# A macaron transformer block on one core: the expert routing computed in two parts, with weight sets behind the gather index

## The chip, the cores and the metric

The kernel runs on one core of one Trainium2 chip. The core has five engines that run beside each other, each through its own instructions in order: TensorE (PE; its weight loads are shown as PEld), VectorE (DVE), ScalarE (ACT), GpSimd (POOL) and SyncE (SP, which here issues transfers only). They meet through semaphores: an instruction increments one when it is done, and another engine waits for a value. The metric is the device time of one execution in microseconds, as a median of runs.

## What is computed

Input is x, 4 sequences of 512 tokens with 128 features, so 2048 tokens in 16 tiles of 128. Six stages follow, each on a layer-normed copy of x:

```python
x = x + 0.5 * ffn(layernorm(x))        # ternary weights, hidden size 512
x = x + attn0(layernorm(x))            # 16 heads of 64, causal, gated
x = x + 0.5 * ffn(layernorm(x))        # the same weights: "the last feed-forward"
x = x + 0.5 * moe(layernorm(x))        # the experts, first time
x = x + attn1(layernorm(x))
x = x + 0.5 * moe(layernorm(x))        # the experts, second time

def moe(X):                            # D = 128, 8 experts, hidden H = 512, top 2
    logits = X @ Wg + bg
    topv, topi = top_k(logits, 2)
    w = softmax(topv)                  # one weight for each of the two experts
    out = X
    for e in range(8):
        for s in range(2):
            xs = X * w[s]
            y = (silu(xs @ W1[e]) * (xs @ W3[e])) @ W2[e]
            out = out + where(topi[s] == e, y, 0)
    return out
```

## The kernel before

x stays in SBUF, tokens on the partitions. Matrix products are made in pairs of 16-bit halves: a number is split in a high and a low f16 part, and three products (high x high, high x low, low x high) are summed in PSUM; ScalarE writes the high parts and VectorE the low ones. PSUM has 8 banks, `ps[:, bank, :]`, of 512 f32 columns.

**Stages and their order.** Each engine has one program, written out by hand, and the order of its calls is the order of its work; no scheduler moves anything. The attention loops over 32 items (4 sequences of 8 head pairs) in 36 turns, as a pipeline of five steps: in turn t the item t is projected, t-1 has its row maxima, t-2 its scores, t-3 its outputs, t-4 its output projection. So turns 32 to 35 have less and less to do. A table `FILL` puts other work in the turns: the feed-forward of sequences 0 to 2 (`up`, `down`) and the router logits (`route(0, 0)`, `route(0, 1)`), and in the second attention `route(1, 0)` to `route(1, 2)`. What concerns the last sequence comes after the attention: `route(0, 2)`, the last feed-forward's `up(1, 3, k)` with VectorE's `hidden_low(1, 3, k)`, `down(1, 3)`, `x_ffn(1, 3)` (adds it to x), `stats(3, 3)`, `normed(3, 3)`, `turned_x(3, 3)` and `route(0, 3)`. After the second attention it is `stats(5, 3)` in turn 35, `normed(5, 3)`, `turned_x(5, 3)` and `route(1, 3)`. In an attention turn VectorE's `turned_low` (L1132) writes the low part of the turned outputs, which PE's `project_out` needs, and `add_out` (L1172) adds its result to x.

**The routing**, `moe(n, m)` on VectorE and `moe(m)` on PE, m = 0 and 1, begins when the logits and top two of all 16 tiles are there. All (token, expert) pairs, 4096, are sorted by expert, each expert's rows padded to whole tiles of 128; this gives up to 39 tiles of rows. The steps on VectorE are `hot` (one-hot of each choice, L1219) and `hoth` (sum of both, L1222); PE multiplies `hoth` by a triangular matrix and by ones and gives each pair's rank in its expert (bank 3) and each expert's count (bank 4). From the counts come the tiles of each expert (L1232 to L1240), from these and the ranks each pair's place (L1242 to L1250): a tile number and a row number in it. `in_row` (L1265) is the one-hot of the row number, `in_tile` the one-hot of the tile number in four versions: itself (L1253), times the token number (L1258), and times the high and low part of the weight (L1261). PE multiplies them (L1653) and gets in bank 5, for each row of each tile, the token, both weight parts and the choice. VectorE turns them into integer rows (`row_i[:, 0]`, the rows to gather, and `row_i[:, 1]`, the rows to scatter) and `wup`, the weights. `tile_ei` holds each tile's expert.

**The tiles.** GpSimd gathers 128 token rows per tile from HBM by an indirect transfer (L702), four ahead, and later scatters the result (L708), 8 tiles behind. PE loads the experts' offsets from `tile_ei` for eight tiles at once (L1663), transposes the gathered rows (L1674), multiplies by both expert matrices (L1366 to L1368), transposes the product (L1696) and multiplies by the third (L1708 to L1710). ScalarE copies the transposed rows (L926) and applies Silu (L932), after it has waited for `wup`.

Two helpers recur. `step(ins)` lets VectorE wait for the instruction just issued, as the next one reads its result:

```python
def step(ins):
    n[0] += 1
    ins.then_inc(chain, 1)
    eng.wait_ge(chain, n[0])
```

## Time and profile before

| | us |
|---|---|
| median of 3 runs | 1029.34 |
| lowest, highest | 1029.19, 1030.26 |
| the profiled execution | 1028.21 |
| its span, first to last instruction | 1026.4 |
| busy in the span: PE, DVE, POOL, ACT | 877.7, 791.5, 699.8, 615.5 |
| first routing, L1214 to L1285 on DVE | 399.05 to 419.08 |
| second routing, L1214 to L1285 on DVE | 882.49 to 902.44 |

The profile is of one execution. A row of the timeline has the start in us from the start of the span, the busy time, the engine, the line in the program, the operation, what it writes and reads, shapes, and how many like it follow each other (x2); in brackets how long the engine was idle before and who released it. The duration of a row with x2 is the busy time of both together.

### The profile page before, as it was taken

Reading aid. Unit: us, or ns where it says so; the run is one execution under the profiler, and the core shown is the slowest. Engines: PE = TensorE matmul, PEld = TensorE weight load, DVE = VectorE, ACT = ScalarE, POOL = GpSimd, SP = SyncE. Lnnn points to the kernel's source line nnn. Section 1 sums busy time; section 2 is a strip of 40 time slices with the busy share of each in tenths; the row PEclk is TensorE's granted clock in tenths of the full one; section 3 lists DMA queues with packets and bytes.
Section 4 is the critical chain, followed back from the end, with each engine's and each line's share of the span. In section 5 each row is a group of like instructions: output and inputs, shape, how many; then the busy total and the mean of one; then the engine's idle time right before and its main releaser. Section 6 shows DMA issues by size and latency. Waiting matters only on the chain.

```text
span 1026.4 us, 30792 instructions
## 1 busy us (share of the span) xinstructions
PE 877.7 (86%) x11902; PEld 615.0 (60%) x11902; DVE 791.5 (77%) x2348; ACT 615.5 (60%) x1024; POOL 699.8 (68%) x638
## 2 busy tenths in 40 slices
PE   5779999999999962699975899999999996189993
PEld 3447667767666641477752567667677665157772
DVE  6778988888889656577776988898888883757774
ACT  6578778778767620266643766666766663046661
POOL 5568899889887740377732887768877876057771
PEclk9899999999999976699996999999999998589997
DMA  4100011010030000111230000000000000011124
GB/s 149 52 34 29 17 44 43 3 43 3 2 103 4 3 11 11 23 53 53 52 103 5 2 2 3 2 12 2 13 3 2 12 3 1 11 36 52 53 50 139
DMA packets 29424, 31.75 MB, mean 31 GB/s; under 512 B 4130, under 2 KB 22306, under 8 KB 29284
## 3 DMA queue, kind: packets, MB, share of 16 engines
q1 hardware_dynamic: 23760, 19.29, 6.3%
q0 software_dynamic: 4992, 10.23, 3.8%
q8 instruction: 99, 1.62, 0.7%
q14 instruction: 41, 0.34, 0.1%
q10 hardware_dynamic: 532, 0.27, 0.1%
HBM read 21.52 MB, written 8.26 MB: 29 GB/s over the span
## 4 chain that ended last, share of the span: by engine, by line
PE 71%; DVE 15%; POOL 5%; ACT 4%; issue 3%; DMA 2%; SPq 0%; POOLq 0%; DVEq 0%; ACTq 0%
PE ps L1548 13%; PE ps L1366 8%; PE ps L1367 8%; PE ps L1368 8%; PE ps L1554 4%; PE ps L1696 3%; PE ps L1571 3%; PE ps L1572 3%; PE ps L1573 3%; PE ps L1516 3%; POOL arena L676 3%; DVE arena L1114 2%; PE ps L1581 2%; PE ps L1708 2%; PE ps L1709 2%
## 5 line engine op out<-in xcount | busy, mean ns | idle before, releaser
L676 POOL TENSOR_TENSOR arena<-arena 128x1024 f16<-128x1024 f32 (+1 forms) x192 | 347.6, 1811 | 106.0 <-ACT arena L843 95.6
L835 ACT ACTIVATE arena<-ps 128x1024 f32<-128x1024 f32 (+1 forms) x192 | 169.2, 881 | 137.3 <-PE ps L1554 136.9
L1114 DVE CUSTOM_DVE_ANT_0 arena<-ps,mask_qk 128x512 bf16<-128x512 f32 (+3 forms) x512 | 224.7, 486 | 23.2 <-PE ps L1516 18.2
L1548 PE MATMUL ps<-arena 64*128 64x512 f16 (+3 forms) x1536 | 149.7, 301 | 11.7 <-ACT arena L835 8.0
L1571 PE MATMUL ps<-arena 128*128 128x65 f16 x1280 | 130.4, 195 | 5.5 <-POOL arena L676 5.5
L702 POOL DMA_INDIRECT arena<-x_rows,arena x78 | 76.5, 980 | 82.3 <-DVE arena L1285 52.6
L1572 PE MATMUL ps<-arena 128*128 128x64 f16 x1280 | 130.5, 194 | 0.0
L1573 PE MATMUL ps<-arena 128*128 128x65 f16 x1280 | 130.2, 194 | 0.0
L1571 PEld LDWEIGHTS ps<-arena 128*128 128x128 f16 x1280 | 118.5, 98 | 5.9 <-POOL arena L676 5.9
L1573 PEld LDWEIGHTS ps<-arena 128*128 128x128 f16 x1280 | 118.0, 98 | 0.0
L1572 PEld LDWEIGHTS ps<-arena 128*128 128x128 f16 x1280 | 117.8, 99 | 0.0
L674 POOL CAST arena<-arena 128x1024 f16<-128x1024 f32 (+1 forms) x128 | 107.2, 838 | 0.0
L708 POOL DMA_INDIRECT y_rows<-arena x78 | 76.8, 985 | 34.9 <-issue 20.1
L1548 PEld LDWEIGHTS ps<-arena 64*128 64x128 f16 x1536 | 57.0, 94 | 65.6 <-ACT arena L835 26.5
L1301 DVE SCALAR_TENSOR_TENSOR arena<-ps,arena 128x512 f32<-128x512 f32 x78 | 58.5, 750 | 36.7 <-ACT arena L932 29.5
L1548 PE MATMUL ps<-arena,sel 64*128 64x512 f16 (+3 forms) x512 | 77.5, 299 | 0.0
L1516 PE MATMUL ps<-arena 64*128 64x512 f16 (+3 forms) x512 | 67.5, 301 | 11.2 <-DVE arena L1114 10.7
L932 ACT ACTIVATE arena<-ps,arena 128x512 f32<-128x512 f32 x78 | 53.7, 689 | 29.8 <-PE ps L1368 29.8
L1307 DVE TENSOR_TENSOR arena<-ps,arena 128x512 f16<-128x512 f32 x78 | 54.0, 692 | 18.6 <-ACT arena L938 18.6
L843 ACT ACTIVATE arena<-arena 128x1024 f16<-128x1024 f32 x64 | 67.4, 1052 | 0.0
L938 ACT ACTIVATE arena<-ps 128x512 f16<-128x512 f32 x78 | 46.6, 597 | 32.2 <-PE ps L1696 32.2
L1554 PE MATMUL ps<-mask_kq,identb 128*128 128x128 bf16 x512 | 62.4, 225 | 0.0
(254 smaller groups left out, 2580.4 us busy)
## 6 DMA issues: line engine op xcount, KB each, us to landing
stage<-in_L_ffn_W SPq DMA_DIRECT2D x4, 1024.0 KB, 5.5
arena<-y_rows SPq DMA_DIRECT2D x16, 256.0 KB, 4.8
x_rows<-XN SPq DMA_DIRECT2D x8, 256.0 KB, 2.3
arena<-x_rows,arena POOLq DMA_INDIRECT x78, 2.5
y_rows<-arena POOLq DMA_INDIRECT x78, 2.3
stage<-in_L_attn_Wkv SPq DMA_DIRECT2D x2, 512.0 KB, 7.9
out_x<-X SPq DMA_DIRECT2D x4, 256.0 KB, 2.9
X<-in_L_attn_tokens SPq DMA_DIRECT2D x3, 256.0 KB, 5.2
```

The source lines that it names most:

```text
L674: g.tensor_copy(PH[:, b, :, cols], P32[:, :, cols]).then_inc(s_ph_pool, 1)
L676: g.tensor_tensor(PL[:, b, :, cols], P32[:, :, cols], PH[:, b, :, cols], ALU.subtract).then_inc(s_pl, 1)
L835: a_.activation(P32[:, :, UNIT_AT[u]:UNIT_AT[u] + UNIT_W[u]], ps[:, 4:6, 0:UNIT_W[u]], ACT.Exp).then_inc(s_ex_p, 1)
L1114: v_.tensor_tensor_reduce(masked[:, x, 0:w], ps[:, 2 + x, at:at + w], mask_qk[:, CH - w:CH], 1.0, NEG, ALU.add, ALU.max, accum_out=MX[:, i ...
L1366: mm(dst, sh, mh, start=True, stop=False)
L1367: mm(dst, sh, ml, start=False, stop=False)
L1516: ins_ = mm(ps[:, 2 + x, at:at + (i + 1) * P], QKh[rows, r, 0, i * P:(i + 1) * P], QKh[rows, r, 1, 0:(i + 1) * P], start=(n_ == 0), stop=( ...
L1548: mm(ps[:, 4 + x, at:at + w], keys, queries, start=(n_ == 0 and part == 0), stop=False)
L1554: ins_ = mm(ps[:, 4 + x, at:at + P], identb[:], mask_kq[:], start=False, stop=(n_ == len(EXP_UNITS[u]) - 1))
L1571: mm(ps[:, 6 + x, c:c + DH + 1], ph_, VH[:, r, k, x, 0:DH + 1], start=(k == 0), stop=False)
L1572: mm(ps[:, 6 + x, c:c + DH], ph_, VL[:, r, k, x, :], start=False, stop=False)
L1573: ins_ = mm(ps[:, 6 + x, c:c + DH + 1], pl_, VH[:, r, k, x, 0:DH + 1], start=False, stop=(k == i))
```

## The change

The 16 tiles are split in EARLY = 12 (three sequences) and TPC = 4 (the last sequence). One-hots, ranks within the expert and the row matrices of the first 12 are computed before the last sequence is routed. To make that possible the row number is taken from the rank alone (rank and 127), and the expert's first tile is added to the tile number afterwards (`first`, `tile_h`). The early part of the first routing lies around the last feed-forward, that of the second in turns 32 to 34 of the second attention. Behind the last sequence's route come its own one-hots, ranks and rows and the two remaining versions of `in_tile`, then the index to gather. The weight versions of `in_tile`, their product (32 matmuls of its own, bank 6) and the rows to scatter now stand behind that index; GpSimd waits for the scatter rows (`s_r_home`) before its first scatter. `in_row` and the small tiles of the early part move to a place in the arena that the attention does not use.

The diff, cut to its core (the functions are also printed above as they were):

```diff
 # GpSimd, scatter(t)
+                    if t == 0:
+                        pool.wait_ge(s_r_home, m + 1)
 # VectorE, attention, end of a turn
+                    if a == 1 and t == ITEMS:
+                        experts_of(0, EARLY)
+                    if a == 1 and t == ITEMS + 2:
+                        early_ranks(1)
+                        rows_of(1, 0, EARLY)
+                        rows_of(0, 0, EARLY)
 # VectorE, new functions
+            def experts_of(lo, hi):
+                for j in range(TOPK):
+                    ins_ = v_.tensor_copy(idxf[:, j, lo:hi], idx8[:, lo:hi, j])
+                step(ins_)
+                for j in range(TOPK):
+                    ins_ = v_.tensor_tensor(hot[:, j, lo:hi], iota_e[:, lo:hi],
+                                            idxf[:, j, lo:hi].unsqueeze(2).broadcast_to([P, hi - lo, EXPERTS]),
+                                            ALU.is_equal)
+                step(ins_)
+                v_.tensor_tensor(hoth[:, lo:hi], hot[:, 0, lo:hi], hot[:, 1, lo:hi], ALU.add).then_inc(s_r_hot, 1)
+            def ranks_of(lo, hi, rank):
+                step(v_.tensor_tensor(prod[:, :, lo:hi].rearrange("p j t e -> p j (t e)"),
+                                      rank.unsqueeze(1).broadcast_to([P, TOPK, (hi - lo) * EXPERTS]),
+                                      hot[:, :, lo:hi].rearrange("p j t e -> p j (t e)"), ALU.mult))
+                step(v_.tensor_reduce(posf[:, :, lo:hi], prod[:, :, lo:hi], AX.X, ALU.add))
+                step(v_.tensor_copy(posi[:, :, lo:hi], posf[:, :, lo:hi]))
+                v_.tensor_scalar(at_i[:, 0, :, lo:hi], posi[:, :, lo:hi], int(math.log2(P)), None, ALU.logical_shift_right)
+                step(v_.tensor_scalar(at_i[:, 1, :, lo:hi], posi[:, :, lo:hi], P - 1, None, ALU.bitwise_and))
+                for k in range(2):
+                    ins_ = v_.tensor_copy(at_h[:, k, :, lo:hi], at_i[:, k, :, lo:hi])
+                step(ins_)
+            def rows_of(j, lo, hi):
+                return v_.tensor_tensor(in_row[:, j * NT + lo:j * NT + hi, :],
+                                        row_no[:].unsqueeze(1).broadcast_to([P, hi - lo, P]),
+                                        at_h[:, 1, j, lo:hi].unsqueeze(2).broadcast_to([P, hi - lo, P]), ALU.is_equal)
+            def early_ranks(m):
+                dve.wait_ge(s_r_rank, 2 * m + 1)
+                ranks_of(0, EARLY, ps[:, 3, 0:EARLY * EXPERTS])
 # VectorE, moe: after the tile totals (in place of L1240 to L1265)
+                ranks_of(EARLY, NT, ps[:, 4, 0:TPC * EXPERTS])
+                for j in (1, 0):
+                    rows_of(j, EARLY, NT)
+                flat = [P, TOPK * NT, EXPERTS]
+                step(v_.tensor_tensor(prod.rearrange("p j t e -> p (j t) e"), hot.rearrange("p j t e -> p (j t) e"),
+                                      cnt[:, 3, :].unsqueeze(1).broadcast_to(flat), ALU.mult))
+                step(v_.tensor_reduce(first, prod, AX.X, ALU.add))
+                step(v_.tensor_tensor(tile_h, at_h[:, 0], first, ALU.add))
+                half = [P, NT, ETILES]
                 for j in (1, 0):
                     blk = slice(j * NT, (j + 1) * NT)
+                    step(v_.tensor_tensor(in_tile[:, blk, 1, :], tile_no[:].unsqueeze(1).broadcast_to(half),
+                                          tile_h[:, j].unsqueeze(2).broadcast_to(half), ALU.is_equal))
+                    v_.tensor_tensor(in_tile[:, blk, 0, :], in_tile[:, blk, 1, :],
+                                     token_1[:].unsqueeze(2).broadcast_to(half), ALU.mult).then_inc(s_r_row, 1)
...
                 dve.wait_ge(s_r_sum, m + 1)
+                step(v_.tensor_scalar(row_f[:, 0, :], ps[:, 5, 0:ETILES], -1.0, 0.0, ALU.add, ALU.max))
+                v_.tensor_copy(row_i[:, 0, :], row_f[:, 0, :]).then_inc(s_r_index, 1)
+                step(v_.tensor_tensor(wts[:, 3, :], wts[:, 1, :], wts[:, 2, :], ALU.mult))
+                step(v_.tensor_copy(wh_r[:, 0], wts[:, 2:4, :]))
+                step(v_.tensor_tensor(wh_r[:, 1], wts[:, 2:4, :], wh_r[:, 0], ALU.subtract))
+                for k in range(2):
+                    v_.tensor_tensor(in_tile[:, :, 2 + k, :], in_tile[:, :, 1, :], w_r[:, k].unsqueeze(2).broadcast_to(every),
+                                     ALU.mult).then_inc(s_r_wset, 1)
...
+                v_.tensor_copy(row_i[:, 1, :], row_f[:, 3, :]).then_inc(s_r_home, 1)
+                dve.wait_ge(s_r_wsum, m + 1)
 # VectorE, between the first attention and moe(3, 0)
             route(0, 2)
+            experts_of(0, EARLY)
             for k in range(FB):
                 hidden_low(1, 3, k)
+            early_ranks(0)
+            rows_of(1, 0, EARLY)
             x_ffn(1, 3)
             stats(3, 3)
             normed(3, 3)
+            rows_of(0, 0, EARLY)
             turned_x(3, 3)
 # PE: early_ranks(1) at the end of turn 33, early_ranks(0) before down(1, 3), early_counts(m) before turned_x
+            def early_ranks(m):
+                pe.wait_ge(s_r_hot, 2 * m + 1)
...
+            def early_counts(m):
...
 # PE, moe
+                pe.wait_ge(s_r_wset, TOPK * (m + 1))
+                for b in range(TOPK * NT):
+                    ins_ = mm(ps[:, 6, 0:2 * ETILES], in_row[:, b, :], in_tile[:, b, 2:4, :].rearrange("p a b -> p (a b)"),
+                              start=(b == 0), stop=(b == TOPK * NT - 1))
+                ins_.then_inc(s_r_wsum, 1)
                 pe.wait_ge(s_r_tile, m + 1)
```

Three places show how the instructions stand. VectorE, from the last `hidden_low` (a low half of the hidden layer, 128x512 x4) to the transposed norm's low part `XTl`, before:

```order
L998 SCALAR_TENSOR_TENSOR arena<-ps,arena 128x512 x4
L1013 SCALAR_TENSOR_TENSOR X<-ps,X 128x512
L975 BN_STATS bst<-X 128x6 x4
L978 BN_AGGR mv<-bst 128x2 x4
L1005 TENSOR_SCALAR XN<-X,mv,rstd 128x128 x4
L992 TENSOR_TENSOR XTl<-ps,XTh 128x512
```

and with the change:

```order
L1007 SCALAR_TENSOR_TENSOR arena<-ps,arena 128x512 x4
L1241 TENSOR_TENSOR arena<-ps,arena 128x2x96
L1244 TENSOR_REDUCE arena<-arena 128x2x12
L1245 CAST arena<-arena 128x2x12
L1246 TENSOR_SCALAR arena<-arena 128x2x12
L1247 TENSOR_SCALAR arena<-arena 128x2x12
L1249 CAST arena<-arena 128x2x12 x2
L1253 TENSOR_TENSOR arena<-row_no,arena 128x1536
L1022 SCALAR_TENSOR_TENSOR X<-ps,X 128x512
```

Seven instructions of ranks and one row matrix now stand ahead of `x_ffn(1, 3)` (X<-ps,X).

VectorE, turns 34 and 35 of the second attention: reciprocal and scaled outputs of the last item, `add_out`, `turned_low`, `add_out`; before:

```order
L1156 RECIPROCAL arena<-ps 128x8
L1160 TENSOR_TENSOR arena<-ps,arena 128x2x4x64
L1172 SCALAR_TENSOR_TENSOR X<-ps,X 128x512
L1132 TENSOR_TENSOR arena<-ps,arena 128x512
L1172 SCALAR_TENSOR_TENSOR X<-ps,X 128x512
L975 BN_STATS bst<-X 128x6 x4
```

and with the change:

```order
L1181 SCALAR_TENSOR_TENSOR X<-ps,X 128x512
L1241 TENSOR_TENSOR arena<-ps,arena 128x2x96
L1244 TENSOR_REDUCE arena<-arena 128x2x12
L1245 CAST arena<-arena 128x2x12
L1246 TENSOR_SCALAR arena<-arena 128x2x12
L1247 TENSOR_SCALAR arena<-arena 128x2x12
L1249 CAST arena<-arena 128x2x12 x2
L1253 TENSOR_TENSOR arena<-row_no,arena 128x1536 x2
L1141 TENSOR_TENSOR arena<-ps,arena 128x512
L1181 SCALAR_TENSOR_TENSOR X<-ps,X 128x512
```

The ranks and both early row matrices stand between the two `add_out`, ahead of the last `turned_low`.

PE, the end of the routing up to the first transposed token tiles, before:

```order
L1647 MATMUL ps<-arena,onesh 128x8 x16
L1653 MATMUL ps<-arena 128x156 x16
L1653 MATMUL ps<-arena 128x117 x16
L1663 TENSOR_LOAD arena
L1674 MATMUL ps<-ident,arena 128x128 x2
```

and with the change:

```order
L1718 MATMUL ps<-arena 128x78 x16
L1718 MATMUL ps<-arena 128x39 x16
L1724 MATMUL ps<-arena 128x78 x32
L1733 TENSOR_LOAD arena
L1744 MATMUL ps<-ident,arena 128x128 x2
```

The 32 weight matmuls are new, and stand ahead of the load of the expert offsets and of the first transpose.

## Rows read from the trace of the kernel before

**Rows 1.** The page: granted clock in 40 slices of the span, tenths of full.

```profile
PEclk9899999999999976699996999999999998589997
```

**Rows 2.** Waits from 395 to 425: who waited for whom, us in total, times, longest.

```profile
POOL arena L702 <- DVE arena L1285: 26.4, 1, 26.4
```

**Rows 3.** Timeline of DVE, the second routing (start, busy time, engine, line, operation).

```profile
882.49 0.19 DVE L1214 TENSOR_TENSOR arena<-top 128x16 f32<-128x16 f32 x1
...
883.41 0.29 DVE L1222 TENSOR_TENSOR arena<-arena 128x128 f16<-128x128 f32 x1
...
885.40 0.17 DVE L1232 TENSOR_SCALAR arena<-ps 128x8 f32<-128x8 f32 x1 [0.68 <-PE ps L1647]
...
886.93 0.17 DVE L1240 TENSOR_SCALAR arena<-arena 128x8 f32<-128x8 f32 x1
...
890.80 1.53 DVE L1258 TENSOR_TENSOR arena<-arena,token 128x624 f16<-128x624 f16 x2
892.25 2.82 DVE L1261 TENSOR_TENSOR arena<-arena 128x1248 f16<-128x1248 f16 x2
894.98 4.49 DVE L1265 TENSOR_TENSOR arena<-row_no,arena 128x2048 f16<-128x2048 f16 x2
899.39 0.48 DVE L1269 TENSOR_TENSOR arena<-tile_no,arena 128x312 f32<-128x312 f16 x1
...
901.32 0.32 DVE L1278 COPY arena<-ps 128x156 f32<-128x156 f32 x1 [0.51 <-PE ps L1653]
...
902.44 0.18 DVE L1285 CAST arena<-arena 128x39 int32<-128x39 f32 x1
```

**Rows 4.** Timeline of PE, the second routing.

```profile
883.75 0.29 PE L1641 MATMUL ps<-arena,before 128*128 128x128 f16 x1 [2.84 <-DVE arena L1222]
...
897.33 3.96 PE L1653 MATMUL ps<-arena 128*128 128x156 f16 x32 [12.04 <-DVE arena L1265]
```

**Rows 5.** Timeline of all engines, from the second routing's first gather.

```profile
902.90 1.11 POOL L702 DMA_INDIRECT arena<-x_rows,arena  x1 [26.28 <-DVE arena L1285]
...
905.67 0.48 PE L1674 MATMUL ps<-ident,arena 128*128 128x128 f32 x1 [4.39 <-DMA arena<-x_rows,arena]
906.25 0.28 ACT L926 ACTIVATE arena<-ps 128x128 f16<-128x128 f32 x1 [23.32 <-PE ps L1674]
...
907.15 0.64 PE L1366 MATMUL ps<-E1h,arena 128*128 x1
```

**Rows 6.** The load of the expert offsets: min/median/max ns, first and last start.

```profile
L1663 PEldq TENSOR_LOAD <-arena x10: 589/594/1071, 417.5 to 980.9; - x10
```

**Rows 7.** Timeline of DVE, from the last hidden_low to the first routing.

```profile
386.93 0.69 DVE L998 SCALAR_TENSOR_TENSOR arena<-ps,arena 128x512 f16<-128x512 f32 x1 [0.30 <-ACT arena L761]
389.75 0.69 DVE L1013 SCALAR_TENSOR_TENSOR X<-ps,X 128x512 f32<-128x512 f32 x1 [2.13 <-PE ps L1391]
...
393.23 1.12 DVE L1005 TENSOR_SCALAR XN<-X,mv,rstd 128x128 f32<-128x128 f32 x4 [1.47 <-POOL rstd L590]
396.25 0.69 DVE L992 TENSOR_TENSOR XTl<-ps,XTh 128x512 f16<-128x512 f32 x1 [1.90 <-ACT XTh L751]
...
399.05 0.19 DVE L1214 TENSOR_TENSOR arena<-top 128x16 f32<-128x16 f32 x1
```

**Rows 8.** Timeline of PE, first expert matmul of the first routing.

```profile
424.45 0.64 PE L1366 MATMUL ps<-E1h,arena 128*128 x1
```

**Rows 9.** Timeline of DVE, turns 34 and 35 of the second attention.

```profile
870.27 0.69 DVE L1172 SCALAR_TENSOR_TENSOR X<-ps,X 128x512 f32<-128x512 f32 x1 [0.35 <-PE ps L1368]
871.55 0.69 DVE L1132 TENSOR_TENSOR arena<-ps,arena 128x512 f16<-128x512 f32 x1 [0.59 <-ACT arena L862]
```

**Rows 10.** Busy time by stretch: length, PE, PEld, DVE, ACT, POOL, granted clock, DMA share, GB/s.

```profile
874.00:880.00 6.00, 1.12 (x4) 0.72 (x4) 2.65 (x13) 0.60 (x1) 1.27 (x2) 0.50 0.15 44
430.00:432.00 2.00, 2.00 (x13) 1.32 (x13) 1.49 (x3) 1.36 (x3) 0.95 (x1) 0.95 0.00 0
910.00:912.00 2.00, 2.00 (x8) 0.75 (x8) 0.95 (x2) 0.83 (x2) 1.20 (x2) 0.63 0.14 35
```

117 lines of the change are left out of this document (54 added, 63 removed).

## The prediction

> **What bounds the kernel now.** I read the times first: 1029.34 us is the median, the profiled execution took 1028.21 us with a span of 1026.4, so differences of the trace are taken off the median unscaled. Next the row of the granted clock over 40 slices: it dips at slices 17 to 19 and 35 to 37, the two places where the experts are routed, once after each attention [rows 1]. The waits around the first one then name who is late: POOL stands 26.4 us before its first gather and is released by DVE's index cast [rows 2]. The timeline of DVE at the second routing shows why. From the first instruction of the routing (L1214, 882.49) to the index cast (L1285, 902.44) DVE hardly pauses: 19.95 us of one chain, in which the two row matrices take 4.4 us and the 32x39 weight sets 2.7 [rows 3]. PE has two bursts in it and otherwise waits for DVE [rows 4]. Then come gather, transpose, ScalarE's copy, and the first expert matmul (L1366) at 907.15, 24.66 after the start [rows 5]. In the first routing the same span is 399.05 to 424.45, or 25.40 [rows 7, 8]. From the first expert matmul on PE has work without end; so what counts in each routing is when that matmul starts, against what is added ahead of L1214.
>
> **The new chain on DVE, T = 0 at L1214.** Durations fit 0.16 us plus one element per 0.96 GHz cycle, in f16 and f32 alike: 8 elements 0.17, two of 624 elements 1.53 together, two of 2048 elements 4.49 [rows 3]. An instruction that waits for the one before adds 0.03; one that doesn't starts some 0.1 before the last one's end.
> - One-hots of one sequence instead of four: the sum matrix is issued at 0.70 (before 0.92) and ends at 0.89. PE starts 0.15 later and has 8 small matmuls in place of 32. From PE's start to DVE's reading 32 matmuls took 1.65 [rows 3, 4]; 8 take a quarter and a little for the fixed part, 0.5: DVE reads the counts at 1.5, before at 2.91. Adding one and the reciprocal end at 1.3 and hide.
> - Tile totals: L1232 to L1240 took 1.53 [rows 3]; the scaling by 128 is gone: 3.04.
> - Ranks of the last sequence: product and sum over 64 elements, 0.26 each, cast 0.21, shift and mask 0.30, two casts 0.30: 1.33, to 4.4.
> - Two row matrices of 512 elements, 0.69 long, 0.62 apart: 1.24, to 5.6. The other 1536 elements of each are elsewhere (below).
> - First tile of each expert: two operations on 256 elements at 0.46 and an add of 0.20: 6.7.
> - Membership: per half 624 elements, 0.84 with its wait, and the token product 0.73 (two of 624 took 1.53 [rows 3]): 3.14, to 9.9. PE multiplies the second half, 16 matmuls of 39 columns, in under 1 us beside what comes next, so DVE's 0.5 wait for the sum goes.
> - Tile experts: from L1269 to the wait before L1278 it was 1.42 [rows 3], the last of which overlaps: to 11.2. Then one operation straight from PSUM and the cast: the index is cast at 11.4 against 19.95, and POOL starts its gather at 11.9 against 20.4 [rows 5]. That is 8.5 us earlier.
>
> **What is queued behind the index.** The first expert matmul does not get these 8.5 us, because the weight sets now stand between. On DVE: three small steps (0.63) from 11.5, two products of 1248 elements (2.83 together, [rows 3]): 15.0. On PE 32 matmuls of 78 columns stand ahead of everything of the tiles. At 1.2 GHz, where 16 of 156 and 16 of 117 columns took 3.96 [rows 4], they need 32 x 0.065 = 2.1: last start 17.1. Behind them in PE's queue is the load of the expert offsets, which took 0.59 to 1.07 [rows 6] and was hidden behind the gather; now it is bare. I take 0.7: transpose of token tile 0 at 17.8. The gather, 2.8 from issue to transpose [rows 5], arrives at 14.7 and is hidden; the second, issued some 1.4 behind it, also. DVE meanwhile makes the scatter rows (0.9), reads the weight sum at 17.4 and is ready at 18.1, when ScalarE may start; the transpose releases it at 17.8 + 0.58 = 18.4. From ScalarE's copy to the first expert matmul 0.90 [rows 5]: 19.3. The gains are 25.40 - 19.3 = 6.1 and 24.66 - 19.3 = 5.4, in all **11.5**. The scatter's new wait on POOL is met: its rows are ready at 16, and the first scatter comes eight gathers later.
>
> **What the moved part costs, first routing.** The early one-hots (0.9) lie between route(0, 2) and the first hidden_low, where DVE waits for ScalarE. PE's 12 early rank matmuls (some 0.5) fit in where it waits for the last hidden_low, and the 24 early count matmuls fall where PE waits for the norm. But DVE's early ranks (product and reduction over 192 elements 0.40 each, the rest 0.82: 1.62) and the first row matrix of 1536 elements (1.67 to the next start) stand between the last hidden_low and x_ffn(1, 3). DVE is free at 387.55 and x_ffn started at 389.75 [rows 7]; now at 387.55 + 3.3 = 390.85. **Cost 1.1**, on the path (x_ffn, statistics, norm, transpose, route). The second matrix of 1.76 falls between the norm's end, 394.3, and turned_x at 396.25 [rows 7]: it just fits. If that cover were gone it would cost up to 1.7 more.
>
> **Second routing.** The early one-hots fit after turn 32. But the rest is issued after add_out of turn 34, and in-order DVE then has 1.62 + 2 x 1.67 = 5.0 ahead of turned_low(31), the last output tile of the last head pair. add_out started at 870.27 and the next can start at 870.9; turned_low started at 871.55 [rows 9]. New: 875.9. **Cost 4.3**, all on the path, since PE's last projection, add_out, statistics and norm follow one from the other. And PE stands idle for those 4.3; its projection moves from before 874 to about 876.6, and from 874 on the clock was at its lower level [rows 10]. Its 12 matmuls of 128 columns then run at 1.2 GHz and not at 2.4: 12 x 0.053 = **0.6** more, 0 if the clock holds or was low already.
>
> **The clock at the first tiles.** In 430 to 432 the granted clock is 0.95 and in 910 to 912 it is 0.63 [rows 10], so it rose to 2.4 GHz at 430.2 and 911.5: 5.75 and 4.35 us after the first expert matmul. All of it ran at half speed. Now the weight matmuls and two transposes run up to 1 us before that matmul. Bounds: nothing counts and both ramps last 5.75, a loss of 0.7; or the clock is up when the tiles begin, a gain of (5.75 + 4.35)/2 = 5.0. I take the mean ramp begun 1 us earlier, half a microsecond in each routing: **1.0**.
> The Trainium skill (TensorE: Matmul & The Clock Gate, What's actually happening) says that the gate follows how busy the array has lately been. By that rule alone the weight matmuls should warm the array and the 5.0 be nearer. The trace is divided: a burst of the same kind, 3.96 us long, was followed by pure waiting for the gather and the tiles began at half speed both times.
>
> **Sum.** 11.5 - 1.1 - 4.3 - 0.6 + 1.0 = 6.5 us: 1029.34 - 6.5 = **1022.8 us**.
>
> **Rivals.**
> - Warm start: the clock is high within half a microsecond of the first tiles. For it, PE now works from 15.0 on with gaps below 1 us; against it, the spread of the two ramps seen. 1029.34 - 5.5 - 5.0 = 1018.8.
> - The tail block is hidden: if something else holds turned_low(31), or the block slides into DVE's earlier waits of turns 33 and 34, the 4.9 goes: 1018. Against it, the queue is in order and the block stands behind add_out.
> - The early part is real but small: the first tile is still held by something that did not move, as the serial weight path being 2.5 us longer in each routing (offset load at its longest 1.07, a second wait on the sum, products slower while PE reads the same tiles). Then about half of the 11.5 stays, against 6.0 of cost: 1028.5.
> - Slower: the 32 weight matmuls stand in PE's queue ahead of every tile. In the rows a matmul lasts 0.31 but the next one starts after 0.13 at 156 columns, which is why I price them at 0.065. If 64 of them went one after the other at 0.31, that is 15.7 more: 1038.5. It decides from 0.065 + 6.5/64 = 0.17 a matmul on. Only the rows of the longer matmuls speak against it.
>
> **How the numbers follow.** Forecast 0.78 (1020.5 to 1026), warm start 0.12, hidden tail 0.03, small gain 0.04, slower 0.03. Each DVE chain may be off by 0.7, 1.4 in all; with the clock at its worst (1.7 below my value) the end above is 1026, and the warm start sets the end below, 1019. By 0.2%, 2.06 us, about what a measurement of this kernel can tell from no change: faster 0.93, within 0.04, slower 0.03.
>
> **What would show it.** The index cast 11.4 after the routing's first DVE instruction instead of 19.95; the first expert matmul 19.3 after it in both routings; a bare offset load of 0.6 to 1.1 behind the weight matmuls; x_ffn(1, 3) later by 1.1; a block of 5.0 on DVE between the last two outputs of the second attention, with PE idle beside it; the clock's rise under 5 us after the first expert matmul. It is wrong if the block is not on the path, if the weight matmuls are more than 0.1 apart, or if the tiles begin at 2.4 GHz.

## Result and profile after

The changed kernel takes 1022.81 us (median of 4 runs, 1020.87 to 1023.76) where the kernel before takes 1029.26 (4 runs, 1028.93 to 1030.26) on the same chip: a ratio of 0.9933, 95% interval 0.9916 to 0.9951. The forecast was 1022.8. Its profiled execution has a span of 1022.0 us, before 1026.4. The kernel was run again later, as f0: 1021.48 against 1029.14, ratio 0.9932 (0.9916 to 0.9947), span 1019.5.

Cut at the same events in each trace, the span divides as follows (T is the first DVE instruction of a routing, L1214 before and L1263 after; all in us, one execution each):

| stretch | before | after | f0 |
|---|---|---|---|
| start to the last hidden_low of the last feed-forward | 386.93 | 387.88 | 386.45 |
| to T of the first routing | 12.12 | 13.15 | 13.15 |
| to the first expert matmul | 25.40 | 18.83 | 18.83 |
| expert tiles, to DVE's last result | 103.01 | 102.22 | 102.16 |
| to DVE's first L1114 (after: L1123) of the second attention | 25.91 | 26.01 | 25.93 |
| to its fourth last add_out | 299.41 | 300.83 | 300.84 |
| to its second last add_out | 17.49 | 16.99 | 16.96 |
| to T of the second routing | 12.22 | 17.07 | 17.07 |
| to the first expert matmul | 24.66 | 18.75 | 18.76 |
| expert tiles, to DVE's last result | 102.27 | 102.11 | 102.07 |
| to the end of the span | 16.96 | 18.17 | 17.28 |

The rows behind it follow. First the page's granted clock in 40 slices, after; it answers to [rows 1]. The dips of the two routings lie at slices 15 to 17 and 35 to 36, before at 15 to 17 and 34 to 36 (the prediction counted them two slices too late, at 17 to 19 and 35 to 37), and they are about as deep as they were. The dip at slices 21 and 22 is the start of the second attention.

```profile
PEclk9899999999999986699987999999999999579997
```

The timeline of DVE after, first routing (start, busy time, engine, line, operation, and in brackets what ended the idle time before it). It answers to [rows 3], which is the second routing; the two run alike within 0.1.

```profile
401.03 0.19 DVE L1263 TENSOR_TENSOR arena<-top 128x16 f32<-128x16 f32 x1
...
402.53 0.17 DVE L1271 TENSOR_SCALAR arena<-ps 128x8 f32<-128x8 f32 x1 [0.23 <-PE ps L1710]
...
412.38 0.18 DVE L1306 CAST arena<-arena 128x39 int32<-128x39 f32 x1
...
413.13 2.83 DVE L1314 TENSOR_TENSOR arena<-arena 128x1248 f16<-128x1248 f16 x2
...
418.31 0.20 DVE L1323 COPY arena<-ps 128x39 f32<-128x39 f32 x1 [1.41 <-PE ps L1724]
...
418.77 0.24 DVE L1325 TENSOR_SCALAR arena<-arena 128x39 f32<-128x39 f32 x1
```

The counts are read 1.50 after T, and the index is cast at 11.35 (11.28 in the second routing, where it was 19.95). The weight sets (L1314) stand behind the cast, and the weight is ready (L1325 ends) at 17.98.

The timeline of the other engines, from the first gather to the first expert matmul, first routing, after. It answers to [rows 4, 5, 8].

```profile
412.87 1.24 POOL L709 DMA_INDIRECT arena<-x_rows,arena  x1 [17.70 <-DVE arena L1306]
...
416.01 2.26 PE L1724 MATMUL ps<-arena 128*128 128x78 f16 x32 [4.34 <-DVE arena L1314]
...
418.07 0.67 PE L1744 MATMUL ps<-ident,arena 128*128 128x128 f32 x2
...
419.05 0.45 ACT L935 ACTIVATE arena<-ps 128x128 f16<-128x128 f32 x2 [17.59 <-DVE arena L1325]
...
419.86 0.60 PE L1408 MATMUL ps<-E1h,arena 128*128 x1 [1.12 <-DVE arena L1331]
```

The gather is issued 5.2 before the transpose (L1744) needs it and is hidden. What releases ScalarE is now DVE's weight, no longer the transpose as in [rows 5]. The load of the expert offsets, to be compared with [rows 6] (min/median/max ns, first and last start):

```profile
L1733 PEldq TENSOR_LOAD <-arena x10: 591/598/1073, 416.9 to 975.4; - x10
```

It starts at 416.9 and, even at its longest, is over by 418.0, while the weight matmuls still run to 418.27. The transposes start directly behind them.

DVE from the last hidden_low to the second row matrix, after, answers to [rows 7]:

```profile
387.88 0.69 DVE L1007 SCALAR_TENSOR_TENSOR arena<-ps,arena 128x512 f16<-128x512 f32 x1 [0.46 <-ACT arena L770]
...
390.06 1.76 DVE L1253 TENSOR_TENSOR arena<-row_no,arena 128x1536 f16<-128x1536 f16 x1
391.74 0.68 DVE L1022 SCALAR_TENSOR_TENSOR X<-ps,X 128x512 f32<-128x512 f32 x1
...
396.24 1.75 DVE L1253 TENSOR_TENSOR arena<-row_no,arena 128x1536 f16<-128x1536 f16 x1
398.23 0.69 DVE L1001 TENSOR_TENSOR XTl<-ps,XTh 128x512 f16<-128x512 f32 x1 [0.23 <-ACT XTh L760]
```

x_ffn (L1022) follows hidden_low by 3.86, before by 2.82. It no longer waits for PE. The second matrix fits with 0.24 to spare.

DVE at the end of the second attention, after, answers to [rows 9]; the last row is PE's, the first matmul of the last output projection.

```profile
865.91 0.68 DVE L1181 SCALAR_TENSOR_TENSOR X<-ps,X 128x512 f32<-128x512 f32 x1
...
868.08 3.43 DVE L1253 TENSOR_TENSOR arena<-row_no,arena 128x1536 f16<-128x1536 f16 x2
871.42 0.68 DVE L1141 TENSOR_TENSOR arena<-ps,arena 128x512 f16<-128x512 f32 x1
...
873.66 0.69 DVE L1181 SCALAR_TENSOR_TENSOR X<-ps,X 128x512 f32<-128x512 f32 x1 [1.56 <-PE ps L1410]
```

```profile
872.16 0.29 PE L1408 MATMUL ps<-WOh,arena 128*128 128x128 f16 x1 [5.46 <-DVE arena L1141]
```

Five microseconds without a pause, and turned_low (L1141) behind them with no wait of its own: this block of ranks and row matrices (the tail block below) is late, nothing else. PE stood idle for 5.46 before its projection.

Busy time by stretch (length, PE, PEld, DVE, ACT, POOL, granted clock, DMA share, GB/s), after; it answers to [rows 10]. The rows are the two ramps (a ramp is the time from the first expert matmul until the clock is at 2.4 GHz) and the projection's window.

```profile
424.00:426.00 2.00, 2.00 (x12) 1.08 (x11) 0.75 (x1) 1.21 (x3) 0.21 (x2) 0.88 0.11 33
904.00:906.00 2.00, 2.00 (x8) 0.75 (x7) 0.95 (x2) 0.30 (x2) 0.94 (x1) 0.56 0.01 2
870.00:874.00 4.00, 1.84 (x32) 1.84 (x33) 2.44 (x3) 0.00 (x0) 0.00 (x0) 0.50 0.01 4
```

The clock rises to 2.4 GHz at 424.5 and 905.8, that is 4.6 and 4.0 after the first expert matmul. In 870 to 874 it is 0.50 throughout; before it was 0.93 in the same window.

### The profile page after: what moved, and what is told of

Same layout as the page of the kernel before. It is cut to its first block, busy times and chain, and to the rows that moved or that the text cites. A ratio compares the mean times of both kernels' runs of the same rounds, so it can differ in the third digit from the quotient of the medians.

```text
span 1022.0 us, 31003 instructions
## 1 busy us (share of the span) xinstructions
PE 876.2 (86%) x11990; PEld 615.3 (60%) x11990; DVE 799.2 (78%) x2382; ACT 615.0 (60%) x1024; POOL 700.3 (69%) x638
## 3 DMA queue, kind: packets, MB, share of 16 engines
q8 instruction: 100, 1.64, 0.6%
## 4 chain that ended last, share of the span: by engine, by line
PE 70%; DVE 15%; POOL 5%; ACT 4%; issue 3%; DMA 2%; SPq 1%; POOLq 0%; DVEq 0%; ACTq 0%
PE ps L1590 12%; PE ps L1408 8%; PE ps L1409 8%; PE ps L1410 8%; PE ps L1596 4%; PE ps L1766 3%; PE ps L1613 3%; PE ps L1614 3%; PE ps L1615 3%; PE ps L1558 3%; POOL arena L683 3%; DVE arena L1123 2%; PE ps L1623 2%; PE ps L1779 2%; PE ps L1778 2%
## 5 line engine op out<-in xcount | busy, mean ns | idle before, releaser
L1123 DVE CUSTOM_DVE_ANT_0 arena<-ps,mask_qk 128x512 bf16<-128x512 f32 (+3 forms) x512 | 224.6, 486 | 24.1 <-PE ps L1558 19.3
L1339 DVE SCALAR_TENSOR_TENSOR arena<-ps,arena 128x512 f32<-128x512 f32 x78 | 58.5, 750 | 38.1 <-ACT arena L941 31.1
L1558 PE MATMUL ps<-arena 64*128 64x512 f16 (+3 forms) x512 | 67.3, 300 | 12.5 <-DVE arena L1123 12.0
```

What stands on the lines that cost most here:

```text
L1123: v_.tensor_tensor_reduce(masked[:, x, 0:w], ps[:, 2 + x, at:at + w], mask_qk[:, CH - w:CH], 1.0, NEG, ALU.add, ALU.max, accum_out=MX[:, i ...
L1558: ins_ = mm(ps[:, 2 + x, at:at + (i + 1) * P], QKh[rows, r, 0, i * P:(i + 1) * P], QKh[rows, r, 1, 0:(i + 1) * P], start=(n_ == 0), stop=( ...
```

## Experiments

All kernels are derived from the changed one. Two chips were used. The first four runs went to a chip on which the kernel before takes 1063.65 us (17 runs), the other six to one where it takes 1029.14 (11 runs; 1028.55 over 8 runs beside the last two). Times are compared by the ratio to the kernel before on the same chip. The changed kernel without an edit was not run on the first chip, so for e4, e5, e1 and e6 its ratio of 0.9933 is carried over from elsewhere, and the main readings rest on distances inside the traces. What the first chip does differently is told under the last heading.

**e4: the split kept, nothing early.** The early part is computed inside the routing, ahead of the last sequence's part, on DVE and on PE.

```diff
-                    if a == 1 and t == ITEMS + 2:
-                        early_ranks(1)
-                        rows_of(1, 0, EARLY)
-                        rows_of(0, 0, EARLY)
...
+                experts_of(0, EARLY)
+                early_ranks(m)
+                rows_of(1, 0, EARLY)
+                rows_of(0, 0, EARLY)
                 experts_of(EARLY, NT)
```

> The same split and the same instructions, but the part of the first 12 tiles is computed at the start of the routing, after the last route, and not beside other work. Theory A, the gain is in hiding that part: one-hots 0.9, ranks 1.6, row matrices 3.4 and a round trip to TensorE of about 0.7 come back, so the first expert matmul is 25.3 us after the routing's first instruction against 18.8; 13 us more in two routings, less the 1.1 and 4.9 that the early part cost elsewhere: 1022.8 + 7 = 1029.8. Rival B, the gain came from putting the weight sets behind the gather index: at most 1025.

Measured: 1066.05 us (10 runs), ratio 1.0024 (1.0011 to 1.0036). The index is cast 18.10 and 18.03 after T, and the first expert matmul comes 25.81 and 25.63 after it. The two costs are gone: x_ffn again 2.82 behind hidden_low, and 12.42 from the second last add_out to T. Theory A put the first expert matmul at 25.3 and the time 7 us above the changed kernel; by the ratios it is 9.7. In the traces the two routings take 13.5 more (against e1) and x_ffn and the end of the attention give 5.7 back, which is 7.8; the other 2 us were not looked for. So the gain is the work moved out of the chain, less what it costs where it was put. Splitting and putting the weights behind the index, without moving anything out, bring nothing; they cost 0.24%.

**e5: the weight sets ahead of the gather index, as before.** The early part stays early.

```diff
+                step(v_.tensor_tensor(wts[:, 3, :], wts[:, 1, :], wts[:, 2, :], ALU.mult))
...
+                    v_.tensor_tensor(in_tile[:, :, 2 + k, :], in_tile[:, :, 1, :], w_r[:, k].unsqueeze(2).broadcast_to(every),
+                                     ALU.mult).then_inc(s_r_wset, 1)
+
                 step(v_.tensor_tensor(tile_e8, tile_no[:].unsqueeze(2).broadcast_to([P, ETILES, EXPERTS]),
```

> The changed kernel with the weight sets computed ahead of the tile experts and of the gather index on VectorE, as in the kernel before. Theory A, in the changed kernel the first tile is released by the weights and not by the gather: the index cast moves from 11.4 to 14.9 us after the routing's start, the gather starts at 15.3, its second transfer lands at 19.7 and the first expert matmul starts at about 19.9 instead of 18.8, so 1.1 us more in each routing: 1025. Rival B, the index was the gain: 3.5 us more in each: 1029.8.

Measured: 1058.39 us (4 runs), ratio 0.9959 (0.9943 to 0.9975). The index falls back by 3.4 (14.75 and 14.67 after T), the weight comes 1.8 earlier, and the first expert matmul is at 20.09 and 19.38 against 19.03 and 18.92 on the same chip with the changed order (e1): 1.1 and 0.5 later, where theory A had 1.1 twice. Timeline of e5, first routing:

```profile
415.86 1.24 POOL L709 DMA_INDIRECT arena<-x_rows,arena  x1 [21.10 <-DVE arena L1315]
...
416.91 0.18 DVE L1326 TENSOR_SCALAR arena<-arena 128x39 f32<-128x39 f32 x1
...
418.62 0.47 PE L1745 MATMUL ps<-ident,arena 128*128 128x128 f32 x1 [2.42 <-DMA arena<-x_rows,arena]
```

Here the weight is ready at 417.1 and PE waits 2.42 for the gathered rows. The two orders hold the first tile by different chains, and they differ by only 0.5 to 1.1, since the gather's 2.8 and the weight's path through PE are of like length. The changed order is the better one because its gather is fully hidden.

**e1: the tail block moved half a turn forward.** In turn 34 ranks and both row matrices go ahead of evacuate, behind the turned_low before.

```diff
+                    if a == 1 and t == ITEMS + 2:
+                        early_ranks(1)
+                        rows_of(1, 0, EARLY)
+                        rows_of(0, 0, EARLY)
                     if v is not None:
                         evacuate()
```

> The changed kernel with one block moved: in turn 34 of the second attention the early ranks and both early row matrices stand ahead of the evacuation of the last item's outputs, where VectorE waited 5.9 us, and no longer behind add_out. Theory A, the block of 4.9 us was on the path and its idle time also put the last projection on the low clock (0.6): from add_out(30) to the first instruction of the routing it takes 12.2 us as before the change, not 17.1, and the kernel takes 1022.8 - 4.9 = 1017.9. Rival B, something else held the last turned_low, so the block was free: 1022.8. Rival C, the block now runs beside GpSimd's subtraction of the exponentials and stretches it, as the 1.95 us cast in turn 32 shows the two engines disturbing each other: the last outputs come up to 2 us later, 1020.

Measured: 1052.69 us (5 runs), ratio 0.9909 (0.9894 to 0.9925) where the changed kernel has 0.9933 and 0.9932: about half of theory A's 4.9. From the fourth last add_out to T it is 30.53 instead of 34.06, so 3.5 come back; against the kernel before (29.71) 0.8 are missing. The timeline of DVE and one row of PE in e1:

```profile
879.06 3.43 DVE L1253 TENSOR_TENSOR arena<-row_no,arena 128x1536 f16<-128x1536 f16 x2
882.40 0.20 DVE L1165 RECIPROCAL arena<-ps 128x8 f32<-128x8 f32 x1
```

```profile
883.39 0.66 PE L1623 MATMUL ps<-ident,arena 128*128 128x128 f32 x4 [2.27 <-DVE arena L1169]
```

The block ends, evacuate (L1165) begins without a wait, and PE stands 2.27 for it (0.36 in the changed kernel). The granted clock belongs to this reading. In e1 it was 1.00 from 873.9 to 884.1, and PE had the last item's outputs ready 14.7 after the fourth last add_out, while the block ended at 16.6: 2.0 late. Before the change most of that turn ran at 0.50 and the outputs were ready at 16.2; there the same block would be 0.4 late (an estimate from these two). Behind it the clock of e1 was 0.50, and the last add_out came 2.25 after turned_low (before 1.62). That 0.63, and 0.18 of a longer wait for ScalarE ahead of turned_low, are the missing 0.8; the second last add_out lies 17.49 behind the fourth last in both. Rival C is not what is seen: GpSimd's tensor instruction at the start of the block takes 1.15 with and without it beside.

**f1: the block spread, and the first routing's row matrix moved.** One row matrix of the second routing goes behind the norm; in the first routing one goes behind the statistics instead of ahead of x_ffn.

```diff
+                        early_ranks(1)
+                        rows_of(1, 0, EARLY)
                     if v is not None:
                         evacuate()
...
-            rows_of(1, 0, EARLY)
             x_ffn(1, 3)
             stats(3, 3)
+            rows_of(1, 0, EARLY)
...
             normed(5, 3)
+            rows_of(0, 0, EARLY)
             turned_x(5, 3)
```

> The changed kernel with its early part spread over VectorE's waits: in the second attention the early ranks and one row matrix stand ahead of the last evacuation (turn 34) and the other behind normed(5, 3); around the last feed-forward the first row matrix stands behind stats(3, 3) and no longer ahead of x_ffn(1, 3). Theory A: from add_out(30) to the routing it takes 12.2 to 12.5 us as before the change (17.1 changed), from the last hidden_low to the routing 12.3 (13.1 changed, 12.1 before); 5.5 us less than the changed kernel of this call. Rival B, POOL's work is stretched by VectorE's beside it: half of that, 2 to 3.

Measured: 1018.70 us (5 runs), ratio 0.9901 (0.9885 to 0.9916), span 1015.0 against 1019.5 of f0. Theory A's 5.5 was missed: by the medians it is 2.8, as in rival B (the profiled execution of f1 was the lowest of its five). At the tail 5.46 come back (28.57 from the fourth last add_out to T, f0 34.03, before 29.71), which is more than the block cost. The same edit in f3 and g1 gives 29.78 and 29.87, so 4.2 are the block's, and T is as far from that add_out as before the change. The other 1.2 of f1 are the clock's: where its dip falls in the last turns is not the same. In f3 DVE waits 1.44 for PE behind the smaller block; in f1, with turn 34 at full clock as in e1, it does not wait and is 0.3 late. Busy time by stretch in turn 34, of f1 and then of f3:

```profile
862.00:864.00 2.00, 1.66 (x45) 1.48 (x41) 1.97 (x3) 0.00 (x0) 0.00 (x0) 1.00 0.00 0
```

```profile
860.00:862.00 2.00, 2.00 (x39) 2.00 (x37) 0.61 (x1) 0.00 (x0) 0.00 (x0) 0.50 0.00 0
```

The first routing loses, though. x_ffn is early again (2.88), yet T comes 13.59 after hidden_low where f0 has 13.15. The timeline of f1 shows why:

```profile
391.38 1.73 DVE L1252 TENSOR_TENSOR arena<-row_no,arena 128x1536 f16<-128x1536 f16 x1
391.55 1.64 POOL L594 TENSOR_SCALAR pw<-mv 128x4 f32<-128x4 f32 x1 [11.79 <-DVE mv L987]
```

POOL's 4-element step ends 0.08 after the row matrix beside which it runs, and the norm waits for it.

**g1: f3 (below) with that one matrix put back ahead of x_ffn.** This tests that reading.

```diff
+            rows_of(1, 0, EARLY)
             x_ffn(1, 3)
             stats(3, 3)
-            rows_of(1, 0, EARLY)
```

> The kernel of f3 with one thing undone: in the first routing the 1536-element row matrix stands ahead of x_ffn(1, 3) again, as in the changed kernel (spread in turn 34 and filler matmuls stay). Theory A, that the row matrix beside POOL's computation of the norm is what cost f1 and f3 0.45 us there: POOL's L594 falls from 1.64 to 0.22, the first routing starts 13.15 after the last hidden_low instead of 13.60, and the time is 0.4 us under f3, 1012.6 where before is 1029.1 (ratio 0.9844), which is less than the intervals can part; the trace has to show it. Rival B, that POOL's 1.64 has another cause: it stays and the routing starts at 13.6 plus the 1.04 that the matrix costs ahead of x_ffn, 14.6, and the time is 1014.

Measured: 1013.12 us (4 runs), ratio 0.9851 (0.9833 to 0.9870), f3 0.9848. The times can't part the two, as expected; the trace does. T is 13.15 after hidden_low (f3 13.60), and the same POOL step in g1 takes:

```profile
393.59 0.22 POOL L594 TENSOR_SCALAR pw<-mv 128x4 f32<-128x4 f32 x1 [12.95 <-DVE mv L987]
```

So it is 1.64 with a row matrix beside it and 0.22 without, as theory A had it. The Trainium skill (SBUF — State Buffer, SBUF: two separate sides) says that VectorE and GpSimd share a pair of ports as an exclusive lock, which a VectorE instruction with two SBUF inputs holds to its end against a GpSimd instruction that reads SBUF. The row matrix has two such inputs, and the ends 0.08 apart agree with it.

**e6: PE kept busy ahead of the weight matmuls.** Nine matmuls of 512 columns whose result nobody reads (fillers below) stand between the token sums and PE's wait for the weight sets.

```diff
+                for _ in range(9):
+                    mm(ps[:, 2, :], XTh[:, 0:P], XTh[:, 0:CH], start=True, stop=True)
                 pe.wait_ge(s_r_wset, TOPK * (m + 1))
```

> The changed kernel with nine extra matmuls of 512 columns on TensorE, between the token sums and the weight matmuls, where it waited 4.3 us for the weight sets; their result is not used. Theory A, what the array did lately decides the clock: weight matmuls and tiles begin at 2.4 GHz, which gives back half of the 4.6 and 4.0 us that the tiles ran at 1.2 GHz and about 1 us at each set of weight matmuls: 1022.8 - 6.3 = 1016.5. Rival B, the clock rises only some 4 us after the tiles begin, whatever came before: 1022.8. In between, it rises within the tiles earlier than before: 1019 to 1021.

Measured: 1056.40 us (6 runs), ratio 0.9930 (0.9910 to 0.9949), as the changed kernel and as rival B had it, but not for its reason: the clock rose at 414.6 and was lost again. PE and DVE of e6, first routing, and busy time by stretch behind it:

```profile
416.37 1.30 PE L1726 MATMUL ps<-arena 128*128 128x78 f16 x32 [1.04 <-DVE arena L1314]
...
419.00 0.20 DVE L1323 COPY arena<-ps 128x39 f32<-128x39 f32 x1 [1.75 <-PE ps L1726]
...
420.50 0.39 PE L1408 MATMUL ps<-E1h,arena 128*128 x1 [2.00 <-DVE arena L1331]
```

```profile
420.00:422.00 2.00, 1.50 (x6) 0.81 (x7) 0.49 (x2) 1.97 (x3) 1.17 (x2) 0.86 0.24 31
422.00:424.00 2.00, 2.00 (x6) 0.60 (x5) 0.95 (x2) 0.54 (x3) 0.95 (x1) 0.50 0.10 35
```

The weight matmuls take 1.30 instead of 2.26, but DVE does not read their sum earlier: 1.3 after PE's modelled end. After 2.0 without work the expert matmuls begin at full speed (0.39), and the clock falls under them at about 421.4 and is 0.50 until after 424.

**f2: PE kept busy in all three of its waits.** Nine such matmuls (warm(n) issues n of them), and four more behind the weight matmuls and four ahead of the first expert matmul.

```diff
+                warm(9)
                 pe.wait_ge(s_r_wset, TOPK * (m + 1))
...
                 ins_.then_inc(s_r_wsum, 1)
+                warm(4)
...
                     k, e = t % 2, offsets[t]
+                    if t == 0:
+                        warm(4)
```

> The changed kernel with unused matmuls of 512 columns in all three of TensorE's waits behind the token sums: nine before the weight matmuls, four behind them, four behind the two token transposes ahead of the first expert matmul. With nine alone the clock did rise, at 414.6, but fell again at 421.4 behind 2.0 us of idling, so that 4 us of the tiles still ran at 1.2 GHz. Theory A, without that gap the clock stays at 2.4 GHz through the first tiles: (4.6 + 4.0)/2 = 4.3 us less than the changed kernel of this call, less 0.5 if the last four overlap the first tile. Rival B, the clock falls whatever fills the gap: no gain, up to 1 us lost.

Measured: 1017.68 us (5 runs), ratio 0.9898 (0.9883 to 0.9914). The first expert matmul comes 0.67 earlier in both routings (18.16, 18.09), and the tiles take 100.68 and 100.46 instead of 102.16 and 102.07 (f0). PE of f2, first routing:

```profile
414.10 1.29 PE L1728 MATMUL ps<-arena 128*128 128x78 f16 x32 [1.18 <-DVE arena L1314]
415.23 1.02 PE L1724 MATMUL ps<-XTh 128*128 128x512 f16 x4
...
416.31 1.03 PE L1724 MATMUL ps<-XTh 128*128 128x512 f16 x4
417.27 0.39 PE L1408 MATMUL ps<-E1h,arena 128*128 x1
```

The granted clock is 1.00 from 413 to 426 without a break. That is a gain of 4.4 in the two routings, where theory A had 4.3; the median shows 3.8.

**g2: the four and four alone, without the nine.**

```diff
-                warm(9)
                 pe.wait_ge(s_r_wset, TOPK * (m + 1))
```

> The changed kernel with 4 unused 512-column matmuls behind the weight matmuls and 4 ahead of the first expert matmul, and not the 9 ahead of the weight matmuls. PE then has work without a gap from the weight matmuls on (416.0 in the first routing), at half clock at first. Theory A, that the clock rises some 4 us after the start of unbroken work whatever it is (in f2 2.5 to 4 us behind the first filler, in the changed kernel 4.0 and 4.6 behind the first expert matmul): it rises at 419.5 to 420.5, at or just behind the first expert matmul, the loops take 101.0 to 101.4 instead of 102.1; the fillers at half clock (0.43 each) end at about 420.3 and so hold the first expert matmul 0.4 us back; whole gain over the changed kernel 0.8 to 1.8 us, about 1020 where before is 1029.1. Rival B, that the clock must be up before the gap to be held through it: it rises as in the changed kernel 4 us after the first expert matmul, and the time is 1022 to 1023, with the fillers' 0.4 lost twice.

Measured: 1022.58 us (5 runs), ratio 0.9944 (0.9930 to 0.9959): nothing gained, and neither theory is right as a whole: the time is rival B's, the clock is theory A's. PE of g2, first routing:

```profile
415.35 2.26 PE L1727 MATMUL ps<-arena 128*128 128x78 f16 x32 [4.34 <-DVE arena L1314]
417.41 1.91 PE L1724 MATMUL ps<-XTh 128*128 128x512 f16 x4
419.11 0.63 PE L1748 MATMUL ps<-ident,arena 128*128 128x128 f32 x2
419.54 1.41 PE L1724 MATMUL ps<-XTh 128*128 128x512 f16 x4
420.79 0.38 PE L1408 MATMUL ps<-E1h,arena 128*128 x1
```

The clock did what theory A said: PE worked without a pause from 415.35, the clock was up at 420.3, ahead of the first expert matmul, and the tiles take 100.60 and 100.30. But the eight fillers make that matmul not 0.4 but 1.58 and 1.32 late: at half clock the first four hold the transposes until 419.1, and the next four wait behind those. Tiles gain 1.56 and 1.77, the start loses 2.90. In f2, behind the nine, the same four and four take 1.02 and 1.03, and the first expert matmul is not late at all.

**f3: f1 and f2 together.** The edits are those of both.

> Both of the two before together. The parts do not touch each other: by theory A of both 5.5 + 4 = 9.5 us less than the changed kernel of this call. If only the spread works, 5.5; if they disturb each other, less than the larger of the two.

Measured: 1013.02 us (5 runs), ratio 0.9848 (0.9831 to 0.9865), span 1011.3. That is 16.1 under the kernel before and 8.5 under the changed one on the same chip (f1 alone gives 2.8, f2 alone 3.8, by medians), where theory A had 9.5.

**f0: the changed kernel again**, without an edit, beside f1 to f3. Its numbers stand under the result.

> The changed kernel itself, beside the others of this call. On the chip of the first experiments the kernel before took 34 us more than on that of the first result, and from the first expert matmul to the last result each expert phase took 119 us in place of 102. Theory A, the gain does not depend on the chip, since neither DVE's chain nor the attention's end differ: 6.5 us less than the kernel before here too. Rival B, it shrinks or grows where the expert loop is slower: outside 5 to 8.

It is 7.7 us less than the kernel before, inside 5 to 8. But this chip runs the kernel before in the same time as the first result's (1029.14 and 1029.26), so rival B, which speaks of a chip with slower expert loops, was not tested.

## Why the prediction was right, and where it was right by luck

- **The chain to the index** held closely: counts at 1.50 (forecast 1.5), index cast at 11.35 (11.4). The work that e4 puts back into it costs 6.7 of the index and 6.8 and 6.7 of the first expert matmul (against e1, on the same chip).
- **Which chain holds the first tile** was right: the weights, not the index. e5 shows it from the other side.
- **First expert matmul:** forecast 19.3, measured 18.83 and 18.75, so the gains are 6.57 and 5.91, in all 12.5 and not 11.5. The mis-sized term is the offset load. The prediction laid it bare behind the weight matmuls at 0.7, so that the transpose would be at 17.8 and ScalarE would start at 18.4. It ran beside them: the transpose started at 17.04, and ScalarE at 18.02, right behind DVE's weight (17.98), forecast at 18.1. So what released ScalarE was the weight, and not the transpose as forecast. The 32 weight matmuls took 2.26 in all (forecast 2.1), so the rival that they stand 0.17 or more apart falls.
- **x_ffn:** forecast 1.1, measured 1.04, and T moved by 1.03. The second matrix fitted as forecast.
- **The tail block:** forecast 4.3 + 0.6. turned_low came 5.51 instead of 1.28 after add_out, which is 4.23, and the next add_out 2.24 instead of 1.62 after it, which is 0.62, with the projection's matmuls 0.10 apart at a granted clock of 0.50. In f3 T is 29.78 behind the fourth last add_out, before 29.71: without the block nothing of it is left.
- **The ramps:** forecast 1.0; the clock rises 4.6 and 4.0 (f0: 4.4 and 4.0) after the first expert matmul where it took 5.75 and 4.35, and the tiles take 0.95 (f0: 1.05) less. The price of a microsecond at half clock, 0.5 in the prediction, was too high: the 4.4 and 4.0 of f0 cost 1.5 and 1.6 of tile time against f2. The prediction's other bound, a warm start, did not come by itself. The weight matmuls did not warm the tiles. The rule that the prediction took from the Trainium skill (TensorE: Matmul & The Clock Gate, What's actually happening), that the gate follows how busy the array has lately been, is borne out by f2, though: with PE at work through the waits the two loops take 4.1 less than before the change, and the first expert matmuls come 1.3 earlier than in the changed kernel, against the 5.0 of that bound.
- **A miss without consequence:** the early one-hots after turn 32 took 3.8 and not 0.9. Timeline of DVE and of POOL, after:

```profile
849.51 1.95 DVE L1230 CAST arena<-idx 128x12 f32<-128x12 uint32 x2
851.49 0.72 DVE L1233 TENSOR_TENSOR arena<-iota_e,arena 128x96 f32<-128x96 f32 x2
852.25 1.09 DVE L1237 TENSOR_TENSOR arena<-arena 128x96 f16<-128x96 f32 x1
```

```profile
849.22 2.13 POOL L683 TENSOR_TENSOR arena<-arena 128x1024 f16<-128x1024 f32 x1
...
852.01 1.21 POOL L683 TENSOR_TENSOR arena<-arena 128x512 f16<-128x512 f32 x1
```

In the first routing, with POOL idle, the same three took 0.25, 0.43 and 0.26. Here the casts end 0.11 after POOL's first tensor instruction and the add 0.12 after its second. The turned_low behind them came 4.35 after add_out instead of 2.55, but the next add_out came 8.11 after it in both kernels, so the delay reached no one.

- **Slips of the prediction without consequence:** besides the slices, its working gives 1019 as the lower end and its range has 1020.5, and the price of the rival with a small gain, redone, is 1027.8 and not 1028.5 (11.5 less 5.0 for two slower weight paths, less 6.0 of cost, and the 1.0 of the ramps).

- **What the sum did not hold:** the terms measured in place give 12.5 + 1.0 - 1.0 - 4.9 = 7.6, against 6.5 forecast; the medians give 6.45 and, in f0, 7.66; the two profiled executions differ by 4.4. Between them stands the second attention, which the change does not touch in its first 32 turns. It needs 1.4 more up to the fourth last add_out, all of it in its first turns: from its first add_out to the fourth last, the distances between add_outs are the same in both kernels. The two turns after that take 0.5 less. Busy time by stretch, first of before, then of after, both from 24.0 behind DVE's first L1114 or L1123 of that attention:

```profile
577.37:579.37 2.00, 2.00 (x32) 1.58 (x28) 2.00 (x9) 1.51 (x2) 1.70 (x5) 1.00 0.00 0
```

```profile
572.09:574.09 2.00, 2.00 (x21) 1.73 (x18) 2.00 (x9) 1.08 (x2) 1.71 (x5) 0.50 0.00 0
```

The same work, 32 matmuls begun at full clock and 21 at half. Before, the dip came earlier:

```profile
571.37:573.37 2.00, 2.00 (x8) 0.80 (x7) 1.97 (x2) 1.40 (x3) 1.92 (x2) 0.50 0.00 0
```

In f1 and f2 this start costs 0.65 more still. As these rows read, a change that shifts everything by some microseconds also shifts where such dips fall, here against it. That it was the dip's place is read from rows of one execution of each kernel (three that agree in the length of this start for the changed order: after, f0 and g2) and was not tested by a run of its own. The end of the span is 1.2 longer after (0.3 in f0) for a cause that was not looked for, and the profiled execution of after was already 0.6 late at the last add_out of the first attention, ahead of any changed instruction, and 0.95 at the last hidden_low.

The forecast so hit the median with its sum 1.1 too small and an unforeseen loss of about 0.9 net in the attention. The mechanisms were right but for the offset load; that the number fits to 0.1 is luck.

## What to carry to other kernels

When a step is taken out of a serial chain, price it where it lands with every instruction it brings, and look for the engine's waits on both sides: here 4.9 of the second routing's 5.9 were lost to a block put ahead of the last turned_low, and the same work in two pieces, half a turn earlier and behind the norm, cost nothing. Then ask what else stands beside it, since a wide two-input VectorE instruction can stretch a tiny GpSimd step on the path by nearly its own length (here by 1.4 of 1.7 us). And where TensorE waits in several short pieces ahead of a long run of matmuls, filling one pause alone (e6, on the other chip) or two (g2) bought nothing, filling all of them bought 4.4 us. The room that DVE has in a turn is not fixed either: it shrank by 1.5 us where the clock was high.

## What the runs showed of the hardware that was not expected

- Where the clock's dips fall goes with 1 to 2 us in this kernel, read from single executions and not tested by itself: in the second attention's first turns (1.4 between before and after, 0.65 more in f1 and f2) and in its last (1.2 between f1 and f3), at the same instructions.
- TensorE's clock was lost under running work. In e6 it fell at 421.4, while expert matmuls ran, after the 2.0 us pause before them; with that pause filled (f2) it stayed at 2.4 GHz.
- Small VectorE steps beside GpSimd's large ones are stretched too. In f3 the shift and mask of 24 integers in turn 34 (L1245, L1246) took 0.18 and 1.13, the mask ending 0.03 after GpSimd's tensor instruction; in the first routing, with GpSimd idle, it took 0.17.
- A semaphore behind matmuls may be seen later than the modelled end. In e6, with the array at full clock and nothing behind the weight matmuls but the offset load and two transposes, DVE read their sum 1.3 after it; in f2, with fillers behind them, and in the changed kernel, at half clock and with nothing behind them, 0.04 after it. Why was not settled. e6 and f2 ran on different chips, and on e6's chip the delay was 0.3 in e1 as well.
- Chips differ by 3.3% on the same program: 1029.1 and 1063.7 us. Nearly all of the difference is in the two expert loops, which take 118 to 121 us in every kernel on the slower chip and 100 to 103 on the other, at the same granted clock (0.98 over the first 100 us of tiles in e1 and in f0) and the same durations of single instructions (0.75 for DVE's L1339 on both). What is longer are pauses between instructions, on all engines. In the first loop of e1 the weight loads of L1408 stand 13.2 us in 26 pauses in which they wait for nothing that the profile shows, in f0 2.6 us in 5. These loops are the ones whose matmuls take their weights at an address read at run time. The cause was not tested. Outside the loops the chips agree: from T to the first expert matmul e1 has 19.03 and 18.92, f0 18.83 and 18.76.
